# A gated cross-attention block on one core: first sample in whole float32 products, raw operands loaded where their low halves go, new engine orders

## The chip, the cores and the metric

One core of one Trainium2 chip runs the whole kernel. The metric is the device time of one execution in microseconds, as the median of several runs. A profiled execution of the same kernel gives the rows that are read below.

## What is computed

Eight samples of `x` and `ctx`, each 256 rows of 1024 values (C = 256, D = 1024), all float32, with small weights. Cut to what matters:

```
xn = layernorm(x)                                  # over the 1024 values
t  = Wt @ ctx ;  p = Wp @ xn ;  g = Wg @ ctx       # (256,256) @ (256,1024)
att = sum over a group of 32 rows of p*g           # one number per group and sample
y  = Wz (block diagonal) @ (att * t)
x1 = x + tanh(g_xattn) * (groupnorm(y)*gn_w + gn_b + ctx)
h  = layernorm(x1)
scores = (h @ Wq.T) @ keys.T                       # 64 experts
gate   = softmax over the 16 best scores, 0 for the others
z   = (h @ A.T) , gated expert by expert (8 columns each)
out = x1 + tanh(g_ffn) * 2 * (z_gated @ B.T)
```

## The kernel before, in words

The kernel rewrites the algebra. `Wu` (the product of Wz and Wt) is made once, and so is a router block (Wq and keys), 64 columns wide, which is put beside the 512 columns of A. Per sample n there are these products on PE:

- `u_product`: Wu times ctx, four uses of 512 columns into `w_ps[0..3]`; `gram`: x times ctx, transposed copies of both as operands, 256 by 256; `ctx_sums`: column sums of ctx; `n_product`: Wp times the corrected gram (`M`); `group_means` and `group_att_var`: averages over groups of 32 rows.
- `hT`: transposes of the attention result for the two row tiles t = 0, 1; `z_product(t, n)`: 8 chunks k of A with the router; `zT`: transposes of the gated z; `out_product(k, n)`: four quarters, each 4 chunks j of B.

A large product is made of three products of float32r operands: every operand v is held as v_hi (v rounded to float32r, by ACT: `xT_high`, `cT_high`, `c_high`, `lot_high`, `M_high`, `hT_high`, `zT_high`) and v_lo = v - v_hi (by DVE or POOL: `xT_low`, `cT_low`, `c_low`, `lot_low`, `M_low`, `hT_low`, `zT_low`), and hi*hi, hi*lo and lo*hi are summed in PSUM. `lot_high(j)` and `lot_low(j)` split one of 16 lots of 128x512 weights, 8 of A and 8 of B (KD = 8, KN = 4). Raw values arrive by DMA in places shared among several tensors: `raw`, `stage` and the working tiles `uw`.

DVE also computes the statistics (`x_stats`, `u_statistics`, `att_reduce`, `group_deviation`, `slopes`), the combination `w_tiles` of attention and residual, the gate (`gate`, a chain of some 11 small operations), `offsets` and the last addition `add_out`. POOL does low halves, the three powers of -1/2 (`x_root`, `y_root`, `w_root`), `x_shift` and `x_add`. ACT also does `u_copy`, `w_square`, `residual`, `scale_ctx` and `exps`.

The order is written out by hand for every engine, each engine being a fixed list that waits on semaphores. The list has a start (sample 0 alone, up to `hT(1, 0)`), a loop over b = 0..6 in which sample b's feed-forward part and sample m = b+1's attention part are interleaved (with b = 0 in special branches, since the weights' lots are still being split), and an end (sample 7 alone). On PE a round of the loop begins with `z_product(0, b)` at L872 and ends with `out_product(3, b)` at L899. SP issues all large DMAs in one queue in program order; a wait of SP holds back every later load.

Names and lines: `load_xT` L172, `load_cT` L179, first transposes L183 and L184, `load_x` L190, `load_c` L196, `load_lot` L213 and L216, POOL's `xT_low` L276, `cT_low` L281, `c_low` L287, `x_add` L299, `y_root` L307, `w_root` L311 and L313; ACT's `xT_high` L358, `cT_high` L364, `c_high` L370, `u_copy` L395, `w_square` L408, `hT_high` L414, `lot_high` L442; DVE's `lot_low` L532, `x_plus_ctx` L540, `x_stats` L547, `w_tiles` L629, `offsets` L633 to L636, `hT_low` L642, `gate` L653 to L677, `add_out` L687, `Wp_lo` L719, the router block's low half L731; PE's `gram` L790, `ctx_sums` L803, `u_product` L821, `n_product` L833, `group_means` L841, `group_att_var` L846, `hT` L860, `z_product` L872, `zT` L886, `out_product` L899, Wu L910, router L916.

The waits of PE's start, which the change replaces:

```
pe.wait_ge(wu_lo_s, 1)
u_product(0)
ctx_sums(0)
gram(0, lambda: None)
group_means(0)
pe.wait_ge(wp_lo_s, 1)
n_product(0)
group_att_var(0)
pe.wait_ge(router_lo_s, 1)
hT(0, 0)
hT(1, 0)
```

## Time and profile before

| | us |
|---|---|
| median of 3 runs (range) | 371.48 (370.81 to 372.13) |
| the profiled execution, device time | 369.46 |
| its span, first to last instruction | 367.6 |
| PE, DVE, ACT, POOL busy in the span | 336.3, 285.3, 159.8, 151.1 |
| start of `z_product(0, 1)`, from which the rounds repeat | 99.48 |

The span is 1.9 us shorter than the device time of the same execution, and that execution is 2.0 us faster than the median. The page's chain of waits puts 75% of the span on PE. In a row of a timeline, a record that says x8 is eight instructions, the first number is when the first starts and the second how long they take together; PE's records overlap, so that the distance from start to start is what a matmul costs. A matmul of whole float32 operands is two records, one of float32r operands is one.

### The profile page before, as it was taken

What the parts mean: (1) busy time and instruction counts of PE and PEld (TensorE: products, weight loads), DVE (VectorE), ACT (ScalarE), POOL (GpSimd) and SP (SyncE); (2) the same over time, 40 slices, a digit from 0 to 9 for tenths busy, and PEclk for the clock granted to TensorE, in tenths of its full rate; (3) what the DMA queues carried; (4) which work ended last, traced back from release to release, by engine and by line L of the source; (5) the groups of instructions that cost most, each with busy time, mean ns of one, the idle gap of its engine ahead of it and who ended that gap; (6) DMA issues with size and microseconds to landing.
All of it is one profiled execution on the core that took longest, in us unless ns stands there. A gap on an engine that the chain in (4) does not pass through costs nothing.

```text
span 367.6 us, 5693 instructions
## 1 busy us (share of the span) xinstructions
PE 336.3 (91%) x2104; PEld 307.9 (84%) x2104; DVE 285.3 (78%) x670; ACT 159.8 (43%) x257; POOL 151.1 (41%) x98
## 2 busy tenths in 40 slices
PE   5972996939699999999999999999999999999996
PEld 5871886728599889988999889988998899988984
DVE  2986489987868896898869896889689895787352
ACT  4690391751823445417612563344541761136110
POOL 0061178524476164553477067526455248000000
PEclk9995698978999999999999999999999999999999
DMA  7970571064721445062804173153606240001102
GB/s 265 406 263 32 203 256 57 0 235 123 247 84 57 171 157 189 0 229 75 270 3 156 74 220 126 59 171 139 206 1 230 67 164 0 2 1 59 57 29 87
DMA packets 14924, 47.50 MB, mean 129 GB/s; under 512 B 1824, under 2 KB 1952, under 8 KB 14896
## 3 DMA queue, kind: packets, MB, share of 16 engines
q1 hardware_dynamic: 14544, 46.93, 36.4%
q8 instruction: 17, 0.28, 0.3%
q10 hardware_dynamic: 352, 0.20, 0.2%
q14 instruction: 11, 0.09, 0.1%
HBM read 38.74 MB, written 8.39 MB: 128 GB/s over the span
## 4 chain that ended last, share of the span: by engine, by line
PE 75%; DVE 12%; DMA 5%; ACT 3%; issue 2%; POOL 1%; SPq 1%; ACTq 0%; DVEq 0%
PE w_ps L899 23%; PE z_ps L872 23%; PE w_ps L790 9%; PE w_ps L821 9%; PE t_ps L860 4%; DVE B_lo L532 3%; PE z_ps L833 3%; DMA uw<-in_cT 3%; PE w_ps L872 2%; PE t_ps L886 2%; DMA raw<-in_xT 1%; DVE u_st L581 1%; DMA raw<-in_cT 1%; PE t_ps L803 1%; DVE x_st L547 1%
## 5 line engine op out<-in xcount | busy, mean ns | idle before, releaser
L276 POOL TENSOR_TENSOR xT_lo<-raw,xT_hi 128x1024 fp32r<-128x1024 f32 x14 | 41.9, 3014 | 37.6 <-ACT xT_hi L358 37.6
L899 PE MATMUL w_ps<-B_hi,zT_hi 128*128 128x512 f32 x128 | 53.5, 418 | 2.4 <-issue 2.4
L899 PE MATMUL w_ps<-B_hi,zT_lo 128*128 128x512 f32 x128 | 50.7, 396 | 0.0
L899 PE MATMUL w_ps<-B_lo,zT_hi 128*128 128x512 f32 x128 | 50.6, 395 | 0.0
L872 PE MATMUL z_ps<-A_hi,hT_hi 128*128 128x288 f32 x224 | 49.2, 302 | 0.0
L872 PE MATMUL z_ps<-A_lo,hT_hi 128*128 128x288 f32 x224 | 48.7, 300 | 0.0
L872 PE MATMUL z_ps<-A_hi,hT_lo 128*128 128x288 f32 x224 | 48.5, 298 | 0.0
L872 PEld LDWEIGHTS z_ps<-A_hi,hT_hi 128*128 128x128 f32 x224 | 37.1, 193 | 0.6
L872 PEld LDWEIGHTS z_ps<-A_hi,hT_lo 128*128 128x128 f32 x224 | 36.8, 192 | 0.0
L872 PEld LDWEIGHTS z_ps<-A_lo,hT_hi 128*128 128x128 f32 x224 | 36.7, 192 | 0.0
L281 POOL TENSOR_TENSOR cT_lo<-raw,cT_hi 128x1024 fp32r<-128x1024 f32 x12 | 28.7, 2392 | 16.6 <-DVE uw L629 16.6
L434 ACT ACTIVATE ex<-sc,neg_max 128x64 f32<-128x64 f32 x16 | 5.6, 348 | 65.6 <-DVE neg_max L657 65.6
L287 POOL TENSOR_TENSOR c_lo<-c_sb,c_hi 128x1024 fp32r<-128x1024 f32 x14 | 33.6, 2424 | 0.0
L307 POOL TENSOR_TENSOR y_rs<-y_ve,minus_half 128x2 f32<-128x2 f32 x8 | 5.9, 740 | 65.6 <-DVE y_ve L616 65.6
L395 ACT ACTIVATE uw<-w_ps,neg_u 128x512 f32<-128x512 f32 x32 | 20.0, 685 | 26.5 <-DVE neg_u L586 26.5
L642 DVE TENSOR_TENSOR hT_lo<-t_ps,hT_hi 128x512 fp32r<-128x512 f32 x32 | 20.6, 683 | 12.7 <-ACT hT_hi L414 12.7
L899 PEld LDWEIGHTS w_ps<-B_hi,zT_hi 128*128 128x128 f32 x128 | 24.5, 191 | 7.1 <-issue 2.5
L414 ACT ACTIVATE hT_hi<-t_ps 128x512 fp32r<-128x512 f32 x32 | 17.5, 595 | 28.3 <-PE t_ps L860 28.3
L899 PEld LDWEIGHTS w_ps<-B_hi,zT_lo 128*128 128x128 f32 x128 | 24.4, 191 | 5.4
L899 PEld LDWEIGHTS w_ps<-B_lo,zT_hi 128*128 128x128 f32 x128 | 24.6, 192 | 4.2
L790 PE MATMUL w_ps<-cT_hi,xT_hi 128*128 128x256 f32 x96 | 27.6, 288 | 0.0
L860 PE MATMUL t_ps<-ident,uw 128*128 128x128 f32 x128 | 18.5, 292 | 9.5 <-DVE A_lo L731 5.7
(147 smaller groups left out, 868.7 us busy)
## 6 DMA issues: line engine op xcount, KB each, us to landing
c_sb<-in_ctx SPq DMA_DIRECT2D x16, 512.0 KB, 4.5
raw<-in_xT SPq DMA_DIRECT2D x16, 512.0 KB, 5.3
x_sb<-in_x SPq DMA_DIRECT2D x16, 512.0 KB, 3.2
out_block<-uw SPq DMA_DIRECT2D x14, 512.0 KB, 2.9
raw<-in_cT SPq DMA_DIRECT2D x12, 512.0 KB, 4.0
uw<-in_cT SPq DMA_DIRECT2D x4, 512.0 KB, 7.9
raw<-in_aT SPq DMA_DIRECT2D x4, 256.0 KB, 5.8
raw<-in_bT SPq DMA_DIRECT2D x4, 256.0 KB, 4.3
```

The source lines that it names most:

```text
L276: pool.tensor_tensor(xT_lo[:, half_of(h), :], raw[:, half_of(h), :], xT_hi[:, half_of(h), :].bitcast(f32), ALU.subtract).then_inc(xT_lo_s, 1)
L281: pool.tensor_tensor(cT_lo[:, half_of(h), :], raw_ctx(n)[:, half_of(h), :], cT_hi[:, half_of(h), :].bitcast(f32), ALU.subtract).then_inc(c ...
L287: pool.tensor_tensor(c_lo[:, t, :], c_sb[:, t, :], c_hi[:, t, :].bitcast(f32), ALU.subtract).then_inc(c_lo_s, 1)
L395: act.activation(uw[n % 2][:, t, cols], w_ps[k][:, :], ACT.Identity, bias=neg_u[:, t:t + 1]).then_inc(u_copied, 1)
L414: act.activation(hT_hi[:, t, g * HALF:(g + 1) * HALF], t_ps[g][:, :], ACT.Copy).then_inc(hT_hi_s, 1)
L532: dve.tensor_tensor(lo, slot(j), hi.bitcast(f32), ALU.subtract).then_inc(lot_lo_s, 1)
L642: dve.tensor_tensor(hT_lo[at], t_ps[g][:, :], hT_hi[at].bitcast(f32), ALU.subtract).then_inc(hT_lo_s, 1)
L790: last = pe.matmul(gram_bank(n, t)[:, 0:C], a[:, k, t * P:(t + 1) * P], c[:, k, :], start=(k == 0 and a is xT_hi and c is cT_hi), stop=(k ...
L821: last = pe.matmul(w_ps[k][:, :], w[:, c, rows], v[:, c, cols], start=(c == 0 and w is Wu_hi and v is c_hi), stop=(c == T - 1 and w is Wu_lo))
L860: last = pe.transpose(t_ps[g][:, k * P:k * P + P], uw[n % 2][:, t, d:d + P], ident[:, :])
L872: last = pe.matmul(banks[i][:, 0:ZH], h[:, t, row], w[:, k, i * ZH:(i + 1) * ZH], start=(k == 0 and h is hT_hi and w is A_hi), stop=(k == ...
L899: last = pe.matmul(w_ps[k][:, :], z[:, t, row], w[:, j, cols], start=(j == 0 and z is zT_hi and w is B_hi), stop=(j == KN - 1 and z is zT_lo))
```

## The change

- Places: the helper `split` gives v_hi a place of its own and lets the raw values and v_lo share one, for A, B, Wp, xT and cT; the low half overwrites its raw values. `xT_first` and `cT_first`, sample 0's transposes, lie where B_hi will be. `c_sb` is two buffers, used alternately. `raw` is gone.
- Sample 0's `u`, `gram` and `n` become single products of whole float32 operands (`first_u`, `first_gram`, `first_n`), with neither hi nor lo halves of ctx, xT, cT, M; Wu and Wp are split later, for sample 1.
- PE: the router's products move behind the first gram, sample 1's `u_product` moves into the start, behind `first_n`; `hT(1, 0)` goes inside `z_product(0, 0)`; round 0 is written out with `n_product(1)` behind `out_product(0, 0)`.
- POOL: low halves in pieces of 512 columns; it splits lots 4 to 7 of A and 0 to 3 of B, DVE the rest. In the rounds, `xT_low` and `cT_low` are interleaved and `cT_low` no longer waits for `w_done`.
- SP: most waits go. Transposes of sample n are loaded once gram(n-1) is done, since their place holds that gram's low halves.
- DVE: `offsets` goes behind the additions of a round.

The diff, cut to its core:

```diff
+        def split(name, shape):
+            hi = sb(f"{name}_hi", shape, f32r)
+            with nc.sbuf_tensor(f"{name}_in", shape, f32) as raw:
+                pass
+            return hi, sb(f"{name}_lo", shape, f32r), raw
...
+            def load_transposes(n):
+                for h in range(NH):
+                    if n >= 2 and h == 0:
+                        sp.wait_ge(gram_done, per_tile(n - 1, T - 1))
+                    sp.dma_start(xT_raw[:, half_of(h), :], xT[n][:, half_of(h), :]).then_inc(xT_in[h], 16)
+                    sp.dma_start(cT_raw[:, half_of(h), :], cT[n][:, half_of(h), :]).then_inc(cT_in[h], 16)
             def load_c(n):
-                    if n > 0:
-                        sp.wait_ge(w_done, per_tile(n - 1, t))
+                    if n > 1:
+                        sp.wait_ge(w_done, per_tile(n - 2, t))
...
             load_c(0)
+            load_x(0)
             load_first_transposes()
-            load_x(0)
+            load_c(1)
...
-            for j in range(KD - 2):
+            for j in range(KD):
                 load_lot(j)
-            load_cT(0, 1)
-            for j in range(KD - 2, KD):
+            load_transposes(1)
+            for j in range(KD, KD + KN):
                 load_lot(j)
             load_x(1)
-            load_xT(1)
-            load_c(1)
-            load_cT(1, 1)
-            for j in range(KD, N_LOTS):
+            for j in range(KD + KN, N_LOTS):
                 load_lot(j)
-            load_xT(2)
+            load_c(2)
             for b in range(NB - 1):
                 if b + 2 < NB:
+                    load_transposes(b + 2)
                     load_x(b + 2)
-                    load_cT(0, b + 2)
-                    load_cT(1, b + 2)
-                    load_c(b + 2)
-                store(b, 0)
                 if b + 3 < NB:
-                    load_xT(b + 3)
-                store(b, 1)
+                    load_c(b + 3)
+                for t in range(T):
+                    store(b, t)
...
             pool.wait_ge(w_done, per_tile(0, T - 1))
+            for j in range(KH, KD):
+                lot_low(j)
             xT_low(0, 1)
+            w_root(0)
+            cT_low(0, 1)
             xT_low(1, 1)
-            w_root(0)
...
+            cT_low(1, 1)
+            for j in range(KD, KD + KN):
+                lot_low(j)
+            x_root(1)
+            x_add(1)
+            y_root(1)
+            pool.wait_ge(w_done, per_tile(1, T - 1))
+            xT_low(0, 2)
+            w_root(1)
+            cT_low(0, 2)
+            xT_low(1, 2)
+            cT_low(1, 2)
+            for m in range(2, NB):
                 x_root(m)
                 c_low(m)
...
+                x_shift(m)
+                if m + 1 < NB:
+                    xT_low(0, m + 1)
+                    cT_low(0, m + 1)
+                y_root(m)
+                if m + 1 < NB:
+                    xT_low(1, m + 1)
                 w_root(m)
-                if nn < NB:
-                    cT_low(1, nn)
+                if m + 1 < NB:
+                    cT_low(1, m + 1)
...
(ACT)
+            act.wait_ge(wu_done, 1)
+            act.activation(Wu_first[:, :, :], ..., ACT.Copy).then_inc(wu_s, 1)
             c_high(0, 0)
             c_high(1, 0)
-            for h in range(NH):
-                xT_high(h, 0)
-                cT_high(h, 0)
...
+            cb_copy(0)
+            scale_ctx(0)
+            for t in range(T):
+                c_high(t, 1)
+            u_copy(0)
+            M_high(0)
...
+            for j in range(KD):
                 lot_high(j)
+            xT_high(0, 1)
+            cT_high(0, 1)
+            xT_high(1, 1)
             hT_high(0, 0)
+            w_square(0)
+            cT_high(1, 1)
+            ...Wp_hi...
+            hT_high(1, 0)
+            u_copy(1)
+            exps(0, 0)
+            act.wait_ge(gram_done, per_tile(0, T - 1))
+            for j in range(KD, KD + KN):
+                lot_high(j)
+            exps(1, 0)
+            zT_high(0, 0)
+            cb_copy(1)
+            scale_ctx(1)
+            M_high(1)
+            for j in range(KD + KN, N_LOTS):
+                lot_high(j)
+            residual(0)
+            zT_high(1, 0)
...
(DVE)
+            lot_low(0)
+            att_reduce(0)
+            lot_low(1)
+            slopes(0, lambda: lot_low(2))
+            w_tiles(0)
+            hT_low(0, 0)
+            lot_low(3)
+            u_statistics(1)
+            hT_low(1, 0)
+            offsets(0)
+            gate(0, 0)
+            ...Wp_lo...
+            x_stats(1)
+            minus_means(1)
+            gate(1, 0, w_ps[NH:USES])
+            zT_low(0, 0)
+            gram_fix(1)
+            M_low(1)
+            group_deviation(1)
+            for j in range(KD + KN, N_LOTS):
                 lot_low(j)
+            att_reduce(1)
+            zT_low(1, 0)
+            slopes(1)
+            w_tiles(1)
...
(PE)
+            first_u()
+            ctx_sums(0)
+            first_gram()
+            group_means(0)
+            ...router...
+            first_n()
+            u_product(1, lambda: group_att_var(0))
             pe.wait_ge(router_lo_s, 1)
             hT(0, 0)
-            hT(1, 0)
-            for b in range(NB - 1):
+            z_product(0, 0, z_ps, lambda: hT(1, 0), KN - 2)
+            pe.wait_ge(u_copied, per_use(1, USES - 1))
+            z_product(1, 0, w_ps[NH:USES])
+            zT(0, 0)
+            gram(1, lambda: ctx_sums(1))
+            group_means(1)
+            out_product(0, 0)
+            n_product(1)
+            zT(1, 0)
+            out_product(1, 0, lambda: group_att_var(1))
+            out_product(2, 0, lambda: hT(0, 1))
+            out_product(3, 0, lambda: hT(1, 1))
+            for b in range(1, NB - 1):
```

## Rows read from the trace of the kernel before

**Rows 1.** Windows: PE, PEld, DVE, ACT, POOL busy (count), PEclk, DMA share, GB/s.

```profile
99.48:139.38 39.90, 39.90 (x263) 36.88 (x262) 33.73 (x81) 17.90 (x30) 20.38 (x12) 1.00 0.37 126
...
339.21:367.60 28.39, 24.99 (x153) 22.23 (x151) 10.77 (x36) 3.28 (x6) 0.00 (x0) 1.00 0.15 56
```

**Rows 2.** Windows of the start: all of it, and four us within it.

```profile
0.00:99.48 99.48, 71.54 (x394) 64.30 (x395) 76.45 (x155) 52.65 (x82) 40.05 (x30) 0.86 0.54 190
...
12.00:16.00 4.00, 4.00 (x16) 3.24 (x16) 3.90 (x4) 2.21 (x3) 0.00 (x0) 1.00 1.03 409
```

**Rows 3.** PE's waits in the whole span: us in total, times, longest.

```profile
PE t_ps L860 <- DVE A_lo L731: 5.7, 1, 5.7
...
PE t_ps L886 <- DVE zg_sb L677: 3.7, 1, 3.7
```

**Rows 4.** PE's timeline: start, us, what [idle before <-releaser].

```profile
4.13 2.04 PE L910 MATMUL z_ps<-uw 128*128 128x128 f32 x8 [4.13 <-DMA uw<-in_wzT]
6.28 3.64 PE L916 MATMUL t_ps<-stage 16*128 16x64 f32 x16
9.85 0.80 PE L821 MATMUL w_ps<-c_hi,Wu_hi 128*128 128x512 f32 x1
...
12.58 0.63 PE L821 MATMUL w_ps<-c_hi,Wu_hi 128*128 128x512 f32 x1
...
13.57 0.39 PE L821 MATMUL w_ps<-c_hi,Wu_hi 128*128 128x512 f32 x1
...
25.64 0.35 PE L833 MATMUL z_ps<-M_hi,Wp_hi 128*128 128x256 f32 x1 [2.19 <-DVE M_lo L573]
...
35.48 1.97 PE L860 MATMUL t_ps<-ident,uw 128*128 128x128 f32 x8 [5.71 <-DVE A_lo L731]
...
44.07 0.42 PE L872 MATMUL z_ps<-A_hi,hT_hi 128*128 128x288 f32 x2
```

**Rows 5.** The chain that ended last: start, us, what.

```profile
30.69 1.09 POOL y_rs L307
...
99.48 6.37 PE z_ps L872 x48
105.85 2.87 PE w_ps L790 x24
108.73 0.44 PE t_ps L803 x4
...
118.86 5.46 PE w_ps L821 x24
124.33 1.43 PE z_ps L833 x12
...
127.92 5.59 PE w_ps L899 x24
...
205.65 0.44 PE t_ps L886 x4
```

**Rows 6.** DVE's timeline.

```profile
38.73 0.68 DVE L532 TENSOR_TENSOR A_lo<-raw,A_hi 128x512 fp32r<-128x512 f32 x1
...
55.07 2.00 DVE L670 TENSOR_TENSOR g_scale<-g_rec,w_rs 128x1 f32<-128x1 f32 x1
...
57.91 5.48 DVE L532 TENSOR_TENSOR B_lo<-stage,B_hi 128x512 fp32r<-128x512 f32 x2
63.31 0.27 DVE L653 TENSOR_SCALAR sc<-w_ps,w_rs 128x64 f32<-128x64 f32 x1
...
65.51 0.88 DVE L677 SCALAR_TENSOR_TENSOR zg_sb<-w_ps,g_scale,eg 128x288 f32<-128x288 f32 x2
...
205.22 0.21 DVE L583 BATCH_NORM_AGGREGATE u_mv<-u_st 128x2 f32<-128x12 f32 x1
```

**Rows 7.** POOL's timeline.

```profile
52.35 4.71 POOL L281 TENSOR_TENSOR cT_lo<-uw,cT_hi 128x1024 fp32r<-128x1024 f32 x2 [1.95 <-ACT cT_hi L364]
```

**Rows 8.** ACT's timeline.

```profile
24.84 1.15 ACT L442 ACTIVATE A_hi<-raw 128x512 fp32r<-128x512 f32 x2
```

More of the change, by code:

```diff
@@ L762, in _ @@
                 w_tiles(m)
-                offsets(m)
                 add_out(0, b)
@@ L769, in _ @@
                 add_out(3, b)
+                offsets(m)
             gate(0, NB - 1)
@@ L779, in _, with first_gram @@
         def _(pe):
+            def first_gram():
+                for t in range(T):
+                    for k in range(KD):
+                        if k % KH == 0 and t == 0:
+                            pe.wait_ge(first_xT_in[k // KH], 16)
+                            pe.wait_ge(first_cT_in[k // KH], 16)
+                            if k == 0:
+                                pe.wait_ge(wu_s, 1)
+                        last = pe.matmul(gram_bank(0, t)[:, 0:C], xT_first[:, k, t * P:(t + 1) * P], cT_first[:, k, :],
+                                         start=(k == 0), stop=(k == KD - 1))
+                    last.then_inc(gram_done, 1)
             def gram(n, between):
@@ L805, in ctx_sums, with first_u, u_product @@
                 last.then_inc(cb_done, 1)
-            def u_product(n):
-                if n >= 2:
-                    pe.wait_ge(M_lo_s, per_tile(n, T - 1))
+            def first_u():
+                pe.wait_ge(wu_s, 1)
+                for k in range(USES):
+                    t, cols = use(k)
+                    for c in range(T):
+                        if k == 0:
+                            pe.wait_ge(c_in[c], 16)
+                        last = pe.matmul(w_ps[k][:, :], Wu_first[:, c, t * P:(t + 1) * P], c_sb[0][:, c, cols],
+                                         start=(c == 0), stop=(c == T - 1))
+                    last.then_inc(u_done, 1)
+            def u_product(n, middle=None):
+                if n == 1:
+                    pe.wait_ge(wu_lo_s, 1)
+                else:
+                    pe.wait_ge(M_lo_s, from_second(n, T - 1))
                 for k in range(USES):
@@ L824, in u_product, with first_n @@
                     last.then_inc(u_done, 1)
+                    if k == 0 and middle:
+                        middle()
+            def first_n():
+                pe.wait_ge(wp_in, 16)
+                pe.wait_ge(M_hi_s, per_tile(0, T - 1))
+                for t in range(T):
+                    for c in range(T):
+                        last = pe.matmul(z_ps[0][:, t * C:(t + 1) * C], Wp_raw[:, c, t * P:(t + 1) * P],
+                                         M_first[:, c, :], start=(c == 0), stop=(c == T - 1))
+                last.then_inc(n_done, 1)
             def n_product(n):
-                pe.wait_ge(M_lo_s, per_tile(n, T - 1))
-                if n > 0:
+                pe.wait_ge(M_lo_s, from_second(n, T - 1))
+                if n == 1:
+                    pe.wait_ge(wp_lo_s, 1)
+                else:
                     pe.wait_ge(zg_done, per_tile(n - 1, T - 1))
@@ L874, in z_product @@
                                              stop=(k == KD - 1 and h is hT_lo))
-                    if gated and k == KD - 3:
+                    if gated and k == at:
                         gated()
```

363 lines of the change are left out of this document (140 added, 223 removed).

## The prediction

> **What bounds the kernel now.** I read the windows first. From 99.48 us on, the kernel repeats a round of 39.9 us in which PE is busy for all of it, six times, and then ends in 28.4 us with 25.0 of PE [rows 1]. Nothing in those rounds waits for anything but PE, and the change takes no product out of them. What it can give back lies before 99.48: there PE is busy 71.5 us of 99.5, and its mean clock is 0.86 [rows 2], which is time at the lower of its two levels (1.2 and 2.4 GHz). The waits name what PE lacked: the low half of the router block before the first transposes, 5.7 us; sample 0's gated z, 3.7 us [rows 3]. PE's timeline shows the start in order: Wu's products end at 6.2, `u_product(0)` begins at 9.85 and runs at the lower clock until about 13.2 (0.63 us a record at 12.58, 0.39 at 13.57), `n_product(0)` begins at 25.64 after a wait of 2.2, the first transposes at 35.48 after 5.7, at the lower clock again, which lasts until 44.07 [rows 4]. So the question is when `z_product(0, 1)` can begin, which is 99.48 now.
>
> **Prices.** At the higher clock two float32 matmuls of 128 columns are four records in 0.44 us (L803 [rows 5]), 0.22 a matmul; 512 columns cost four times that, 0.87, and 256 columns 0.44; at the lower clock twice as much. Three float32r matmuls of 512 columns cost 3 x 5.46/24 = 0.68, the gram's three of 256 columns 3 x 2.87/24 = 0.36 [rows 5]. The whole-value products thus cost 8 x 0.19 + 16 x 0.08 + 4 x 0.08 = 3.1 us more of PE; they save no PE time, only the waits for halves. A 512-column copy on ACT takes 0.58 us [rows 8], a 1024-column one twice that; a low half of 1024 columns on POOL 2.36 [rows 7], a piece of 512 1.2 (estimate, half of it; unsplit overhead could make it 1.4); a lot's low half on DVE 0.68 when nothing is in its way, as at 38.73 [rows 6]. `z_product` is 6.4, `out_product` 2.8, `n_product` 1.4, `zT` 0.4 [rows 5]; eight transposes took 1.97 at the lower clock [rows 4], so 1.0.
>
> **The start, step by step** (us from the span's start).
> 1. ACT copies Wu as its first work: 6.2 + 0.6 + a little = 6.9, against 9.85 before, since the router's products (3.64) and the halves of Wu and ctx no longer stand ahead. `first_u` is eight matmuls. In the trace the clock rose some 3.5 us after dense work began at 9.85, and 8.6 after 35.48, where transposes with gaps came first [rows 4]. I take 4: 4.1 us at 1.74 do 2.4 matmuls, 5.6 more cost 4.9: end at 15.9 (15.3 for a rise at 10; 20.8 with none).
> 2. `ctx_sums` 0.4, `first_gram` 16 x 0.44 = 7.0: 23.3. The gram ended at 23.4 before (25.64 less its wait), so the early start pays just for the dearer matmuls. The first transposes land behind x now; at 409 GB/s [rows 2] the 1 MB more ahead of them is 2.6 us, and they are not wanted before 16.3.
> 3. `group_means` 0.4 and the router at half of 3.64 = 1.8: 25.5. M takes that time anyway (wait of 2.2 before). `first_n` 1.8: 27.3.
> 4. `u_product(1)` 5.5 with `group_att_var(0)` (0.4) in it: 33.2. Under it runs the chain that was bare before: variance, POOL's power (1.09 [rows 5]), slope, then `w_tiles` 2 x 1.3, first tile by 32.7, second by 33.9. This moves 5.5 us of `u_product(1)` into PE's holes and keeps the clock up.
> 5. `hT(0, 0)` 1.0: 34.2. ACT reaches it late: router copy from 25.5, eight lots 4.6, three copies of 1024 columns 3.4, so 34.2; copy 0.6, DVE's low half 0.7: `z_product(0, 0)` begins at 35.7, PE idle 1.5.
> 6. 6.4 and `hT(1, 0)` 1.0: 43.1. POOL's lots 4 to 7 run from 33.9, 4 x 1.2 = 38.7, wanted from about 39.8: hidden by a us.
> 7. `z_product(1, 0)` wants `u_copy(1)`: on ACT 1.2 + 2.3 + 1.1 + 0.6 + 1.2 + 2.3 after 34.2, about 43: no wait. End 49.5.
> 8. `zT` 0.4, gram(1) and its sums 6.2: 56.1. Its halves on POOL are three and a half further low halves and `w_root`, ready at 49.2.
> 9. DVE: gate(0, 0) from 43.1, 3.1 us when free (63.31 to 66.4 [rows 6]) and up to 2 x 1.2 of blocking, 48.6; Wp's low half, `x_stats` and its small ones 4.0, 52.6; gate(1, 0) 3.1 + 2.0, 57.7; `zT_low` 0.7: `out_product(0, 0)` begins at 58.4, PE idle 1.9.
> 10. 2.8 + 1.4 + 0.4 + half an `out_product` 1.4: 64.4. DVE: M 2.0, deviation 0.6, lots 12 to 15 4 x 1.0, `att_reduce` 0.8: 65.8, PE idle 1.4. Then 0.3 and 2.8: 68.9.
> 11. Slope by 68.1, first tile 69.4: idle 0.5. `hT(0, 1)` 1.0 and 2.8: 73.2. ACT squares until 72.9, copy and low half until 74.2: idle 1.0; 1.0 and 1.4 more: `z_product(0, 1)` begins at **76.6**, 22.9 earlier. Idle in all 6.3, the uncertain term: 0 if nothing blocks, twice if everything is late.
>
> **Blocking between DVE and POOL.** A small DVE operation, one column wide, took 2.00 us at 55.07, and two lots took 5.48 at 57.91 instead of 1.36, both while POOL made low halves of 1024 columns [rows 6, 7]. The change halves POOL's pieces, so a blocked operation should lose up to 1.2 rather than 2.4, but gives POOL eight lots more; `offsets` moves off the way before the transposes.
> The Trainium skill, page SBUF — State Buffer, section Who interferes with whom, says that a DVE instruction with two SBUF inputs and a GpSimd instruction that reads SBUF exclude each other, whoever starts first keeping the port for its whole instruction. The trace agrees as far as it goes, and the rule speaks against giving POOL more.
>
> **The rounds.** POOL has 20.4 us of work in 39.9 [rows 1] and gets at most six more instruction starts; SP loads sample m+1's transposes only after gram(m), 12.6 into the round; 2 MB at 409 GB/s is 5.1, with issue some 20; ACT copies at 20.6 to 22.6 behind `exps(1, b)`, POOL's two first low halves 21.6 to 26.4; `y_root` is wanted at 29.3. Next late would be `y_root` and with it `hT(0, m)`; cover 2.9 there and some 2 more behind. But these low halves now collide with gate(1, b) and the mean's chain: u's statistics ended at 205.43 and PE wanted them at 206.1 [rows 5, 6], 0.7 of cover against a block of 1.2. Bounds 0 and 0.8 a round; I take 0.3, nearer the free end as only one or two operations can be hit, over five rounds 1.5. A gain there is excluded: PE has no idle time in them. The end is unchanged.
>
> **Sum.** -22.9 + 1.5 = -21.4. The profiled execution took 369.46 (span 367.6): 348.1. The median is 2.0 above it: 371.5 - 21.4 = **350.1**.
>
> **Rivals.**
> - Blocking as often as it can (0.16). Some ten two-input operations stand on DVE between 43 and 66; if each waits out a piece, 12 us instead of my 6, PE's start of the round moves to about 82: 355.5. For it: 57.91. Against: POOL has gaps after 56.
>   By the rule on the Trainium skill's page SBUF — State Buffer (section Who interferes with whom) this is what steady POOL work brings.
> - Dense float32 does not raise the clock (0.07). `first_u` ends at 20.8, sums and gram double to 15: 35.7, `first_n` too; 13 us later than in step 3, then float32r work raises it: 363. For it: no row shows a rise within float32 work. Against: PE streams without a gap there.
> - **Slower** (0.04): the shared place of raw and low halves. If the transposes come so late that POOL's pair ends after y's variance, `y_root`, `w_tiles` and `hT(0, m)` slide, and PE idles each of five rounds. It decides when the pair ends after about 31 instead of 26.4; to eat 22.9 us it must lose 4.6 a round, the pair ending near 36, loads 9 us later than worked out: 373. Against: the queue is 0.37 busy in a round [rows 1].
> - Forecast as above, idle between 0 and 12 (0.73).
>
> **Range and chances.** Below: no idle at all would give 343.8. Above: the first rival with 0.6 a round more reaches 358.5. The second rival and the slower one stay out, 0.11, and some of the tails. A measurement tells 0.3% (1.1 us) from no change. Faster 0.95, same 0.01, slower 0.04.
>
> **What would show it.** Right: `z_product(0, 1)` begins at 74 to 80; float32 records of `first_u` change pace near 11; gram(0) ends near 23; no clock at 0.5 after; six intervals of 39.9 to 40.7. Wrong: records of the first gram 0.44 us apart instead of 0.22 (second rival); DVE operations of small tiles above 1.2 us in a row (first); a round above 42 with POOL's power as releaser (slower).

## The result, and the profile after

The changed kernel takes 345.36 us (median of 4 runs, 345.08 to 345.52), the kernel before, on the same chip, 371.14 us (370.39 to 372.13): a ratio of 0.930, 95% interval 0.928 to 0.933. The profiled execution took 345.4 us, its span is 343.6 us, 24.0 less than before.

The page of the kernel after: busy time of each engine, the clock in 40 slices (here and above as its column gives it), and the chain that ended last, by engine.

```profile
PE 331.4 (96%) x2076; PEld 298.6 (87%) x2076; DVE 253.6 (74%) x656; ACT 155.1 (45%) x254; POOL 155.7 (45%) x148
...
PEclk9999999999999999999999999999999999999999
...
PE 85%; POOL 9%; issue 2%; ACT 1%; DVE 1%; DMA 1%; POOLq 0%; DVEq 0%
```

PE is busy 96% of the span. Before, it was 336.3 of 367.6, or 91%. So its work fell by 5 us, which I read as less time at the lower clock (the mean granted clock of the whole execution is 0.963 before and 1.000 after), less what whole values cost, and its idle time by 19. The chain is on PE for 85% instead of 75%.

The windows, columns as in [rows 1]: the start, two rounds, the end.

```profile
0.00:75.39 75.39, 66.55 (x366) 55.09 (x367) 56.94 (x138) 48.17 (x79) 42.62 (x44) 1.00 0.70 255
75.39:115.37 39.98, 39.98 (x262) 36.88 (x262) 33.35 (x81) 17.93 (x30) 25.52 (x23) 1.00 0.39 134
115.37:155.35 39.98, 39.98 (x262) 36.87 (x262) 30.85 (x81) 17.86 (x30) 19.51 (x18) 1.00 0.38 132
315.25:343.60 28.35, 24.97 (x153) 22.24 (x151) 11.07 (x39) 4.08 (x6) 0.00 (x0) 1.00 0.15 56
```

All of the gain is in the first row. The start took 99.48 us [rows 2] and takes 75.39; the six rounds took 239.73 us (99.48 to 339.21) and take 239.86 (75.39 to 315.25), the end 28.39 and 28.35 [rows 1]. DMA share times length is 54 us before and 53 us now: the same bytes, packed closer. The first round still has 2.5 us more of DVE work and 6 of POOL's than a later one.

PE's waits, all that the view lists: us in total, times, longest.

```profile
PE z_ps L964 <- DMA uw<-in_wzT: 4.4, 1, 4.4
PE w_ps L953 <- DVE zT_lo L653: 1.8, 1, 1.8
PE z_ps L926 <- DVE hT_lo L648: 1.0, 1, 1.0
PE w_ps L839 <- ACT products L448: 0.7, 1, 0.7
PE t_ps L899 <- DVE att_var L597: 0.7, 1, 0.7
PE t_ps L913 <- DVE uw L635: 0.3, 1, 0.3
```

The waits of [rows 3], 5.7 for the router block's low half and 3.7 for sample 0's gated z, are gone. What is left after Wu is 4.5 us in all.

PE's timeline of the start (some rows of it; those of `first_n`, `hT` and later group several records):

```profile
26.35 1.97 PE L872 MATMUL z_ps<-zg_sb,Wp_in 128*128 128x256 f32 x8
27.97 0.58 PE L859 MATMUL w_ps<-c_hi,Wu_hi 128*128 128x512 f32 x1
...
33.90 1.03 PE L913 MATMUL t_ps<-ident,uw 128*128 128x128 f32 x8
35.91 0.53 PE L926 MATMUL z_ps<-A_hi,hT_hi 128*128 128x288 f32 x2 [0.98 <-DVE hT_lo L648]
...
49.65 0.60 PE L940 MATMUL t_ps<-ident,zg_sb 128*128 128x128 f32 x4
...
58.54 0.50 PE L953 MATMUL w_ps<-B_hi,zT_hi 128*128 128x512 f32 x1 [1.80 <-DVE zT_lo L653]
...
69.11 1.09 PE L913 MATMUL t_ps<-ident,uw 128*128 128x128 f32 x8 [0.33 <-DVE uw L635]
...
75.22 0.43 PE L926 MATMUL z_ps<-A_hi,hT_hi 128*128 128x288 f32 x2
```

Two rows of `first_u` alone, split where the records' pace changes (columns: PE busy with its count, PEld busy, PEclk, DMA share, GB/s):

```profile
7.10:12.90 5.80, 5.80 (x7) 2.52 (x8) 1.00 1.03 397
12.90:17.00 4.10, 4.10 (x10) 1.52 (x8) 1.00 1.02 411
```

Seven records in the first 5.8 us are 0.83 us each, ten in the next 4.1 us are 0.41 (one lies on the cut): by their pace the lower level, then the higher. The PEclk column says 1.00 in both, so at the start the pace of the records has to be read, not the column.

Who holds up the start? The chain of waits over that stretch, by line, for the kernel before and then the kernel after (the view cuts the row off):

```profile
by line: DVE B_lo L532 11.6%; DMA uw<-in_cT 9.7%; issue 8.4%; DMA raw<-in_xT 5.3%; DVE u_st L581 4.9%; PE w_ps L899 4.3%; DMA raw<-in_cT 3.9%; PE t_ps L860 3.2%; DVE x_st L547 2.4%; POOL xT_lo L276 2.4%; ACT stage L408 2.3%; DVE g_scale L67
```

```profile
by line: PE w_ps L839 13.1%; PE z_ps L798 9.2%; issue 8.5%; POOL A_lo L267 7.3%; POOL cT_lo L260 7.3%; POOL xT_lo L260 6.6%; POOL B_lo L267 6.6%; POOL c_sb L293 6.6%; PE w_ps L953 5.5%; ACT A_hi L445 4.8%; DMA uw<-in_wzT 4.7%; DVE uw L635 3
```

Before, loads of transposes are 18.9% of 99.48 us, 18.8 us. In order of time they are these:

```profile
3.56 9.69 DMA uw<-in_cT
39.81 5.25 DMA raw<-in_xT
88.25 3.87 DMA raw<-in_cT
```

The first is sample 0's, issued at 3.56 without a wait for any place. Only the other two, 9.1 us, were held back until a shared place came free. After, the one load in the chain is `wzT`, 3.5 us.

The chain after must be read with care: it passes through POOL's low halves only across 4.66 us of "issue" from 62.15. POOL's own timeline shows what it waited for there:

```profile
66.84 0.70 POOL L303 TENSOR_TENSOR y_rs<-y_ve,minus_half 128x2 f32<-128x2 f32 x1 [4.69 <-DVE y_ve L622]
```

It was DVE. So the shares of `A_lo`, `xT_lo`, `cT_lo` and `B_lo` do not show that POOL holds up the start; what PE itself waits for is what the list of waits says, DVE's results.

### The profile page after: what moved, and what is told of

It reads as the page before. It is cut to its first block, busy times and chain, and to the rows that moved or that the text cites. A ratio compares the mean times of both kernels' runs of the same rounds, so it can differ in the third digit from the quotient of the medians.

```text
span 343.6 us, 5669 instructions
## 1 busy us (share of the span) xinstructions
PE 331.4 (96%) x2076; PEld 298.6 (87%) x2076; DVE 253.6 (74%) x656; ACT 155.1 (45%) x254; POOL 155.7 (45%) x148
## 4 chain that ended last, share of the span: by engine, by line
PE 85%; POOL 9%; issue 2%; ACT 1%; DVE 1%; DMA 1%; POOLq 0%; DVEq 0%
PE z_ps L926 24%; PE w_ps L953 24%; PE w_ps L814 10%; PE w_ps L859 10%; PE t_ps L913 4%; PE w_ps L839 3%; PE z_ps L885 3%; PE z_ps L798 2%; PE w_ps L926 2%; PE t_ps L940 2%; POOL A_lo L267 2%; POOL cT_lo L260 2%; POOL xT_lo L260 1%; POOL B_lo L267 1%; POOL c_sb L293 1%
## 5 line engine op out<-in xcount | busy, mean ns | idle before, releaser
L260 POOL TENSOR_TENSOR xT_lo<-xT_in,xT_hi 128x512 fp32r<-128x512 f32 x28 | 35.6, 1295 | 48.9 <-ACT xT_hi L358 46.1
L953 PE MATMUL w_ps<-B_hi,zT_hi 128*128 128x512 f32 x128 | 52.8, 413 | 1.8 <-DVE zT_lo L653 1.8
L926 PE MATMUL z_ps<-A_hi,hT_hi 128*128 128x288 f32 x224 | 48.5, 298 | 1.0 <-DVE hT_lo L648 1.0
L926 PEld LDWEIGHTS z_ps<-A_hi,hT_hi 128*128 128x128 f32 x224 | 36.3, 189 | 1.8 <-DVE hT_lo L648 1.2
L260 POOL TENSOR_TENSOR cT_lo<-cT_in,cT_hi 128x512 fp32r<-128x512 f32 x28 | 36.1, 1312 | 0.0
L279 POOL TENSOR_TENSOR c_lo<-c_sb,c_hi 128x512 fp32r<-128x512 f32 x24 | 30.1, 1287 | 0.0
L953 PEld LDWEIGHTS w_ps<-B_hi,zT_hi 128*128 128x128 f32 x128 | 24.1, 188 | 6.4 <-DVE zT_lo L653 2.3
L953 PEld LDWEIGHTS w_ps<-B_lo,zT_hi 128*128 128x128 f32 x128 | 24.1, 189 | 4.1
L814 PE MATMUL w_ps<-cT_hi,xT_lo 128*128 128x256 f32 x96 | 27.1, 283 | 0.0
L814 PE MATMUL w_ps<-cT_lo,xT_hi 128*128 128x256 f32 x96 | 27.1, 283 | 0.0
L659 DVE TENSOR_SCALAR sc<-z_ps,w_rs 128x64 f32<-128x64 f32 x14 | 4.0, 284 | 31.0 <-PE z_ps L926 30.4
L693 DVE SCALAR_TENSOR_TENSOR uw<-w_ps,tg,uw 128x512 f32<-128x512 f32 x32 | 23.2, 743 | 4.5 <-PE w_ps L953 4.3
```

The source lines that it names most:

```text
L260: last = pool.tensor_tensor(lo[:, chunks, :], came[:, chunks, :], hi[:, chunks, :].bitcast(f32), ALU.subtract)
L279: last = pool.tensor_tensor(c_lo[:, t, cols], c_sb[n % 2][:, t, cols], c_hi[:, t, cols].bitcast(f32), ALU.subtract)
L693: dve.scalar_tensor_tensor(uw[n % 2][:, t, cols], w_ps[k][:, :], tg2[:, 0:1], uw[n % 2][:, t, cols], ALU.mult, ALU.add).then_inc(out_added, 1)
L814: last = pe.matmul(gram_bank(n, t)[:, 0:C], a[:, k, t * P:(t + 1) * P], c[:, k, :], start=(k == 0 and a is xT_hi and c is cT_hi), stop=(k ...
L926: last = pe.matmul(banks[i][:, 0:ZH], h[:, t, row], w[:, k, i * ZH:(i + 1) * ZH], start=(k == 0 and h is hT_hi and w is A_hi), stop=(k == ...
L953: last = pe.matmul(w_ps[k][:, :], z[:, t, row], w[:, j, cols], start=(j == 0 and z is zT_hi and w is B_hi), stop=(j == KN - 1 and z is zT_lo))
```

## The experiments

All were timed beside the kernel before. "z(0,1)" is the start of `z_product(0, 1)`, read from the chain, 75.39 in the kernel after. The gain of the start is called by its suspected parts: u in the gap, pieces, clock, whole values, the late loads as a danger.

**u_late**: sample 1's `u_product` goes back behind gram(1), and with it `u_copy(1)` on ACT and `u_statistics(1)` on DVE; the rest stays.

```diff
-            u_product(1, lambda: group_att_var(0))
+            group_att_var(0)
...
             gram(1, lambda: ctx_sums(1))
+            u_product(1)
             group_means(1)
```

> The changed kernel with sample 1's u product put back behind gram(1), so that nothing stands under sample 0's chain from n to the first transposes. Theory A (the gain is work of sample 1 moved into PE's holes): PE idles 4 to 5.5 us before the first transposes at about 33.9, the clock may fall, and 5.5 us of u come back after gram(1), of which the 1.8 us wait for zT_low covers a part: 349 to 353 us. Theory B (the gain is the whole-value products of sample 0, which are unchanged here): within 1 us of 345.4. Theory C (most of the gain is the clock): 352 to 357, as z_product(0, 0) would run at the lower clock again.

349.54 us (348.86 to 350.65), ratio 0.941 (0.939 to 0.944): 4.2 slower than the kernel after. z(0,1) at 79.34. The waits that come back:

```profile
PE t_ps L915 <- DVE uw L635: 4.0, 2, 3.7
...
PE t_ps L895 <- DVE u_mv L587: 1.0, 1, 1.0
...
```

```profile
26.00:39.00 13.00, 7.77 (x37) 6.83 (x36) 8.70 (x19) 11.57 (x19) 6.76 (x6) 0.74 1.04 400
```

PE is busy 7.8 of 13 us there, at a clock of 0.74 (waits first, then the window of 26 to 39 us). So `u_product(1)` in the gap is worth 4 us, part as filled idle time, part as clock: theory A's range, at its lower end.

**single_ctx**: as u_late, and each load of ctx waits for the sample before, as in the kernel before, at its old place in SP's queue; the halves of sample 1's ctx are made later accordingly.

```diff
-                    if n > 1:
-                        sp.wait_ge(w_done, per_tile(n - 2, t))
+                    if n > 0:
+                        sp.wait_ge(w_done, per_tile(n - 1, t))
```

> Edit: the part two ctx buffers undone in effect: each load of ctx waits until the sample before it has used its tiles, as in the kernel before, at the place in SyncE's queue that it had there. The second sample's u product then can't stand in the gap of the first and goes behind gram(1), as in the run called u_late (349.5 us); its two high halves on ScalarE and low halves on VectorE move to 40 to 46 us. Theory A (the second buffer is worth what the u product in the gap is worth, and nothing in the rounds): 349.5 us to 352 us, with the rounds at 39.98 us. Rival B (the late ctx loads are worth much by themselves: they land behind the weights' lots, and the 4.6 us of low halves fall on a VectorE that is busy there): 353 to 358 us, with a wait of TensorE of 3 us or more for u or the sums of ctx near 53 us. Rival C (they cost in the rounds): rounds over 40.3 us.

353.54 us (352.00 to 355.01), ratio 0.953 (0.948 to 0.958): 8.2 slower than after and 4.0 slower than u_late by the medians; z(0,1) at 82.00, the next round 39.96. Its four runs fall in two pairs, 352.0 and 352.1, 355.0 and 355.0. The profiled one is of the faster pair, and beside u_late's it is 2.7 slower, in the time and in z(0,1). So the late loads of ctx cost some 2.5 us beyond u_late in the faster pair and 5.5 in the other.

```profile
...
PE t_ps L894 <- DVE u_mv L586: 2.5, 1, 2.5
PE w_ps L860 <- DVE zg_sb L682: 1.0, 1, 1.0
```

The median lies in rival B's range and the faster pair at the top of A's. By the waits it is nearer to B, though not by B's own sign: the waits for u's statistics and for gated z are 3.5 us, not one wait of 3, and they come from DVE, where the two low halves of ctx now take 3.7 us at 48.0. Rival C is out: the second buffer costs or gives nothing in the rounds. I read its worth as this, that ctx is there early, so that both its low halves and `u_product(1)` fit where DVE and PE are free.

**whole_pieces**: POOL's low halves of ctx and of the transposes and `x_add` in instructions of 1024 columns again; the weights' lots stay at 512.

```diff
-                return [slice(i * HALF, (i + 1) * HALF) for i in range(NH)]
+                return [slice(0, D)]
...
-                for i in range(2):
-                    chunks = slice(h * KH + 2 * i, h * KH + 2 * i + 2)
+                for chunks in (half_of(h),):
```

> The changed kernel with POOL's low halves and x_add in instructions of 1024 columns again (lots stay at 512). Theory D (blocking by the length of POOL's instruction): DVE's blocked operations in the start, which lose some 8 us in all at up to 1.1 us each, lose up to 2.3 each; those between 49 and 58 us go straight into PE's wait for zT_low: 346.5 to 348.5, and DVE operations of a few columns that take 2 us or more. Theory A (only the work's place counts): within 0.6 us of 345.4.

353.11 us (352.36 to 354.31), ratio 0.953 (0.949 to 0.957): 7.8 slower, far above what I had expected. The trace says how. DVE's timeline of whole_pieces:

```profile
78.98 2.26 DVE L638 TENSOR_TENSOR kappa<-gnb_t,beta 128x2 f32<-128x2 f32 x1
81.16 2.43 DVE L639 TENSOR_TENSOR kappa<-u_dev,slope 128x2 f32<-128x2 f32 x1
...
90.14 2.00 DVE L675 TENSOR_TENSOR g_scale<-g_rec,w_rs 128x1 f32<-128x1 f32 x1
```

And POOL's and PE's at the same time:

```profile
78.81 2.42 POOL L259 TENSOR_TENSOR xT_lo<-xT_in,xT_hi 128x1024 fp32r<-128x1024 f32 x1
81.16 2.41 POOL L259 TENSOR_TENSOR cT_lo<-cT_in,cT_hi 128x1024 fp32r<-128x1024 f32 x1
```

```profile
93.11 0.66 PE L939 MATMUL t_ps<-ident,zg_sb 128*128 128x128 f32 x4 [2.35 <-DVE zg_sb L682]
```

```profile
93.70:101.70 8.00, 8.00 (x50) 7.99 (x49) 4.07 (x6) 1.17 (x3) 0.63 (x1) 0.79 0.94 327
```

Two operations of two columns, 0.19 and 0.14 us in the kernel after, took 2.26 and 2.43, each until POOL's instruction ended; `g_scale` took 2.00 instead of 0.94. DVE was so late in the gate that PE waited 2.35 us in the first round, and after that wait its clock was 0.79 over 8 us. That makes 4.3 us (the first round took 44.31 us instead of 39.98), and the start is 2.8 later as well (PE's first record of `z_product(0, 1)` at 78.04 instead of 75.22), with new waits of PE of 0.9 us before `first_n` and 1.6 before `group_means(1)`. After the first round each is 40.10 instead of 39.98. POOL's work itself is cheaper in whole instructions (2.40 for 1024 columns, 2 x 1.30 in pieces). So the piece's length sets what one collision costs, and it counts in the start and in the first round's gate.

**before_pieces**: the kernel before with POOL's work in pieces of 512.

```diff
-                pool.tensor_tensor(xT_lo[:, half_of(h), :], raw[:, half_of(h), :], ...
+                for i in range(2):
+                    chunks = slice(h * KH + 2 * i, h * KH + 2 * i + 2)
+                    last = pool.tensor_tensor(xT_lo[:, chunks, :], raw[:, chunks, :], ...
```

> The kernel before with POOL's low halves and x_add in instructions of 512 columns, nothing else. In its start DVE operations lose about 18 us to blocking (for instance 2.2 of 2.35, 2.1 of 2.32, 4.1 of 5.48), and with the holes filled it hardly gained, so its start hangs on DVE's chain. Theory D: half of the blocking that lies on the chain goes, 365 to 369. Theory A: PE's order and the serial loads bind, 370 to 372.

367.60 us (366.49 to 369.06) against 371.17, ratio 0.993 (0.990 to 0.996): 3.6 faster than before, in theory D's range; z(0,1) is at 97.20 instead of 99.48, 2.3 earlier in the profiled executions. Pieces alone give 3.6 us before and 7.8 in the new order. That the new order leaves DVE and PE less slack, and that a late DVE there also costs the clock, is my reading of the difference; no run separates the two.

**lots_dve**: all 16 low halves of lots on DVE, none on POOL.

```diff
-            for j in range(KH, KD):
-                lot_low(j)          # POOL
...
-            lot_low(3)
+            for j in range(3, KD):
+                lot_low(j)          # DVE
...
+            for j in range(KD, KD + KN):
+                lot_low(j)
```

> The changed kernel with all 16 lots' low halves on DVE, none on POOL. Theory A: DVE's chain is what PE waits for at two places. Four lots of A (2.7 us) before u_statistics(1) delay hT_low(1, 0) and the mean of u, four of B (2.7 us) go straight into the wait for zT_low: 348 to 351. Theory D (blocking between DVE and POOL is what costs, so less on POOL is better): 345.4 or less.

346.73 us (346.12 to 347.10), ratio 0.933 (0.931 to 0.936): 1.4 slower.

```profile
PE w_ps L925 <- ACT uw L393: 1.3, 1, 1.3
...
PE t_ps L892 <- ACT cb_sb L377: 0.6, 1, 0.6
```

Two waits of 1.3 and 0.6 us are new, that for `u_copy(1)` on ACT among them, and one of 0.5 for B's low half. z(0,1) is at 76.59, 1.2 later, though `first_u` took 8.68 us instead of 9.90 in this execution. So POOL's share of the lots is worth 1.4 by the medians and at most 2.4 by these rows, less than the 3 to 6 I gave it. Theory D, no loss at all, is out as well.

**gram_three**: sample 0's gram as three products of halves again; ACT makes four high and DVE four low halves for it.

```diff
-                        last = pe.matmul(..., xT_first[:, k, ...], cT_first[:, k, :],
-                                         start=(k == 0), stop=(k == KD - 1))
+                        for a, c in ((xT_hi, cT_hi), (xT_hi, cT_lo), (xT_lo, cT_hi)):
+                            last = pe.matmul(..., a[:, k, ...], c[:, k, :], ...
```

> The changed kernel with sample 0's gram made of three float32r products of split operands, its raw transposes in the places of sample 1's. ACT's four copies and DVE's four low halves go into the idle stretch from 9.7 to 17.5 us. Theory A: PE saves 16 x (0.43 - 0.36) = 1.1 us of gram, the halves are ready at 18.7 for the second half of the chunks, sample 1's transposes still land before ACT wants them near 31: 344 to 346. Theory B (whole values are what helps, since splits stand in the way): 4 us or more slower, gram(0) ends at 27 or later.

347.63 us (347.40 to 347.96), ratio 0.936 (0.935 to 0.938): 2.3 slower, between the two expectations. PE's timeline:

```profile
22.32 0.28 PE L903 MATMUL t_ps<-u_mv,group_mean 128*128 128x2 f32 x2
22.53 1.99 PE L986 MATMUL t_ps<-stage 16*128 16x64 f32 x16
25.74 3.75 PE L882 MATMUL z_ps<-zg_sb,Wp_in 128*128 128x256 f32 x8 [1.22 <-ACT zg_sb L386]
```

DVE's timeline:

```profile
20.84 3.43 DVE L724 TENSOR_TENSOR c_lo<-c_sb,c_hi 128x1024 fp32r<-128x1024 f32 x2
24.19 0.87 DVE L575 SCALAR_TENSOR_TENSOR z_ps<-cb_sb,neg_x,z_ps 128x256 f32<-128x256 f32 x2
```

The gram ends at 22.3, 1.9 us earlier than with whole values (0.7 of it because `first_u` took 9.18 us in this execution instead of 9.90), but its correction on DVE (the second row) stands behind the low halves of sample 1's ctx, which end at 24.2, as they end at 24.8 in the kernel after. So M is hardly earlier, PE idles 1.22, and then `first_n` takes 3.75 us instead of 1.97, at a granted clock of 0.50. Whole values save no time on PE; they keep it busy while DVE and ACT do other things. The edit also holds sample 1's transposes back until this gram is done; PE's later waits are those of the kernel after (1.0 for `hT`, 1.8 for `zT`), so that costs nothing that shows.

**before_filled**: the kernel before, with 108 filler matmuls where PE idles in the start, their results unused.

```diff
+            def fill(count, bank):
+                for i in range(count):
+                    pe.matmul(bank[:, 0:C], Wu_hi[:, 0, 0:P], Wu_hi[:, 1, :], start=True, stop=True)
```

> The kernel before with filler matmuls (float32r, 256 columns, into idle banks, results unused) in the holes of its start: 42 in the hole before the first transposes, 24 before zT(0, 0), 42 around group_means(1). All waits stay as they were; only the clock is kept up. Theory C: most of the 24 us is the clock, so this reaches 355 or less. Theory A: the low stretches cost half of about 8 us at 35 to 44, 3 at 58 to 61 and 4 at 81 to 85, less what the waits behind take back: 364 to 368.

369.62 us (367.50 to 371.35, 10 runs) against 371.27, ratio 0.996 (0.994 to 0.999).

```profile
0.00:100.81 100.81, 81.20 (x501) 73.49 (x502) 76.95 (x155) 54.01 (x85) 40.15 (x30) 0.97 0.54 191
```

The clock of the start is 0.97 instead of 0.86 [rows 2], PE is busy 81 us instead of 72, and z(0,1) is at 100.81 (this execution is the slowest of the ten). By the medians the clock alone gives 1.7 us, less than either theory gave it: with PE faster, it only waits longer for DVE, ACT and the loads. So the 24 us are not a matter of the clock alone. The fillers held nothing up where they stand: before the first transposes PE still waits 1.5 us for DVE, before `zT(0, 0)` 1.0, before `group_means(1)` 0.5.

**warm**: the kernel after, with 6 filler matmuls of whole float32 before Wu and 2 before `first_u`.

```diff
+            pe.wait_ge(ident_done, 1)
+            for i in range(6):
+                pe.matmul(t_ps[1][:, 0:P], ident[:, :], ident[:, :], start=True, stop=True)
             pe.wait_ge(wt_in, 16)
...
+            for i in range(2):
+                pe.matmul(t_ps[1][:, 0:P], ident[:, :], ident[:, :], start=True, stop=True)
             first_u()
```

> The changed kernel with six filler matmuls of float32 (128 columns) on PE before the first weights land and two between Wu and first_u, results unused. In the changed kernel the first 6.8 of 16 records of first_u run at the lower clock, until 12.9 us, which costs 2.9 us. If the rise comes a fixed time after dense work begins, it comes 2.7 us earlier and saves 1.4: 344.0. If it comes at a time of its own, no difference: 345.4. Theory C, by which the clock decides elsewhere too, would not change this number.

343.08 us (342.57 to 345.26), ratio 0.927 (0.922 to 0.932): 2.3 faster than after by the medians, where 1.4 was expected; the intervals of the two ratios overlap, so the size is uncertain.

```profile
6.91 7.36 PE L839 MATMUL w_ps<-c_sb,products 128*128 128x512 f32 x16
...
21.67 1.99 PE L980 MATMUL t_ps<-stage 16*128 16x64 f32 x16
23.63 2.93 PE L872 MATMUL z_ps<-zg_sb,Wp_in 128*128 128x256 f32 x8
```

`first_u` takes 7.36 us instead of 9.90. In this execution, the slowest of its four (345.26), part was lost again behind the router's thin products: PE did not wait, and still `first_n` took 2.93 instead of 1.97 (granted clock 0.68 from 23.6 to 26.0).

**late_loads**: the slower rival made real. From sample 2 on, the transposes' loads also wait for the `z_product(1, ...)` that follows the gram.

```diff
                         sp.wait_ge(gram_done, per_tile(n - 1, T - 1))
+                        sp.wait_ge(z_done, per_tile(n - 2, T - 1))
```

> The changed kernel, in which sample m+1's transposes wait in every round also for z_product(1, m-1), 6.8 us later than gram(m) (19.4 into the round instead of 12.6). The cover worked out in the prediction is 4.6 us for POOL's pair of low halves before y_root is late: by it ACT's first copy moves from 20.6 to about 23.5, the pair ends near 30 instead of 26.4, and a round loses 0 to 1.5 us: 345.4 to 353. If there is no such cover, each of five rounds loses the 6.8: 379. If the loads have much more room than that, 345.4.

355.28 us (354.65 to 357.85), ratio 0.960 (0.955 to 0.965): 9.9 slower, in rounds of 41.95, 42.20 and 41.94 us; 0 to 1.5 a round and at most 353 in all were expected. z(0,1) is untouched, 75.53.

```profile
PE w_ps L954 <- ACT uw L398: 4.8, 5, 1.5
...
```

```profile
141.45 1.06 ACT L359 ACTIVATE xT_hi<-xT_in 128x1024 fp32r<-128x1024 f32 x1 [3.35 <-DMA xT_in<-in_xT]
144.00 1.06 ACT L365 ACTIVATE cT_hi<-cT_in 128x1024 fp32r<-128x1024 f32 x1 [1.49 <-DMA cT_in<-in_cT]
144.96 2.41 ACT L398 ACTIVATE uw<-w_ps,neg_u 128x512 f32<-128x512 f32 x4
```

The waits come first, then ACT's timeline in a round that begins at 117.48. The first load is issued 19.46 us into the round instead of 12.60, 6.9 later, and that costs 2.0 to 2.2 a round. If a delay beyond the cover counts in full, the cover in the kernel after is 4.6 to 4.9 us (an estimate from this one delay; no second one was tried). What is late is ACT: it waits 3.35 and 1.49 us for the loads, and `u_copy` of the sample, which PE's `out_product` needs, stands behind the two copies. POOL's `y_root` still waits 1.43 us for DVE, at 31.6 us into the round: it is not what decides. The delay was mis-priced, and the instruction too.

**wp_behind, router_within, three_edits**: attempts on the waits that are left. Wp's low half behind `M_low(1)`; the router's products one by one between the gram's; both, with the fillers of warm.

```diff
-            dve.wait_ge(wp_hi_s, 1)          # Wp_lo
...
             M_low(1)
+            dve.wait_ge(wp_hi_s, 1)          # Wp_lo, three lines
```

```diff
                         last = pe.matmul(gram_bank(0, t)[:, 0:C], xT_first[:, k, ...], cT_first[:, k, :], ...)
+                        if t == 1:
+                            r = pe.matmul(t_ps[0][:, k * NE:k * NE + NE], wq_sb[:, k * P:k * P + P], keys_sb, ...)
```

> Edit: the low half of Wp (one DVE instruction, 0.95 us at 48.13 in the profile of the changed kernel) is moved from in front of the statistics of x of the second sample to behind M_low(1). Theory A (the start is a chain on VectorE that ends at zT_lo, for which TensorE waits 1.8 us before out_product(0,0)): the wait falls to about 0.85 us and the kernel gains 0.95 us, 344.4 us. Rival B (what is gained there only moves to the next wait, for att_var or uw, since DVE then is as late at 66 us as before): 345.2 to 345.6 us, no change. n_product(1) needs the low half only after out_product(0,0), 5.8 us of matmuls, so it should not wait.

> Edit: the 8 thin matmuls of the router (16 records of 64 columns on 16 partitions, 1.99 us between the gram of the first sample and first_n) are put one by one between the matmuls of the gram's second tile. Their work is unchanged. The M that first_n waits for then is ready about 2 us later relative to TensorE's last work, so A (the start is bound by TensorE's own work, and M is ready 1 us or more before first_n asks): the same 345.4 us, within 1. B (the router covers the chain from the gram's end to M, and out of its place that chain is bare; the router's own time in the gram pushes M 2 us later): TensorE waits 1 to 2.5 us before first_n and, after such a gap, runs first_n and part of the u product at the lower clock: 347 to 350 us.

> Edit: both of the above (Wp's low half later, the router within the gram), and the filler matmuls of the run called warm (343.1 us). Sum of the parts if they are independent: 345.4 - 2.3 (warm) - 0.95 (Wp) + what the router within the gram gives. With A for both: 342 us. If the router was needed in its place (B): 344 to 346 us.

wp_behind: 344.93 us (343.76 to 347.52), ratio 0.929 (0.925 to 0.933), not told from the kernel after, and so between A's 344.4 and B's 345.2 to 345.6 without deciding. Its waits for `zT_lo`, `att_var` and `uw` are 1.5, 0.8 and 0.4 us instead of 1.8, 0.7 and 0.3, 0.1 less in all where A had 0.95: Wp's low half takes 1.17 at its new place and the small operation behind it 1.07, both beside POOL. By these waits it is rival B. The profiled execution is the slowest of the four, with z(0,1) at 77.51, and what makes it slow is the clock, in a place that the edit does not touch:

```profile
26.62 3.56 PE L872 MATMUL z_ps<-zg_sb,Wp_in 128*128 128x256 f32 x8
```

`first_n` took 3.56 us instead of 1.97 behind the router's products, with no wait before it, and `first_u` 10.12.

router_within: 347.87 (347.51 to 350.48), ratio 0.939 (0.935 to 0.944), 2.5 slower, in the range of B, but not by B's clock:

```profile
22.64 0.43 PE L804 MATMUL t_ps<-stage 16*128 16x64 f32 x2
...
23.63 0.43 PE L804 MATMUL t_ps<-stage 16*128 16x64 f32 x2
...
27.85 1.97 PE L880 MATMUL z_ps<-zg_sb,Wp_in 128*128 128x256 f32 x8 [0.51 <-ACT zg_sb L387]
```

The rows show thin records and `first_n`; the gram's two records stand between the thin ones. A pair of thin records and a pair of gram records cost 0.99 us from start to start; apart, the router's two cost 0.25 and the gram's two 0.43, so the switch costs 0.3 us a turn, 8 times, 2.5 us. The wait before `first_n` is 0.51, and `first_n` keeps its 1.97. three_edits: 346.11 (345.79 to 346.75), ratio 0.933 (0.931 to 0.936): warm's gain less this loss. The lowest median stays warm's.

## Why the prediction was right, and where it was off

The forecast was 350.1 us, within 343.5 to 358.5; 345.36 came. The gain lies before `z_product(0, 1)`, as said, and by the steps that were named. From the span's start, forecast and timeline:

| | forecast | measured |
|---|---|---|
| 1: `first_u` ends | 15.9 | 16.8 |
| 2: first gram ends | 23.3 | 24.2 |
| 3: `first_n` begins, `u_product(1)` begins | 25.5, 27.3 | 26.35, 27.97 |
| 4, 5: `hT(0, 0)`; `z_product(0, 0)`, PE idle | 33.2; 35.7, 1.5 | 33.90; 35.91, 1.0 |
| 7: `zT(0, 0)` | 49.5 | 49.65 |
| 9: `out_product(0, 0)`, PE idle | 58.4, 1.9 | 58.54, 1.8 |
| 10, 11: idle for `att_var`, `uw`, `hT` | 1.4, 0.5, 1.0 | 0.7, 0.3, 0 |
| `z_product(0, 1)` | 76.6 | 75.39 |
| a round (mean of six before: 39.96) | 39.9 + 0.3 | 39.98 |

- **The start**, -22.9 forecast and -24.1 measured. Step 1 had the rise of the clock 4 us after dense work began; it took 5.8 us, which cost 0.9. Steps 3 and 4 gave back 0.2 and step 5's idle time was 0.5 shorter, so that steps 7 and 9 fit within 0.15 in part because two misses cancel, and steps 10 and 11 gave back the rest: 1.0 us of waits in place of 2.9, with 0.6 more of work. Idle in all was 3.8 us (the 0.7 for Wu's copy was in step 1), not 6.3. The wait named last, for `hT(1, 1)`, did not come. Two of the signs that were named came late: the pace of `first_u` changed at 12.9, not near 11, and gram(0) ended at 24.2, not near 23.
- **The rounds**, +1.5 forecast, +0.1 measured over the six intervals (239.86 against 239.73). In this term I had charged blocking to PE. It does take place: in the round from 115.37, `slope` took 1.23 us, the two tiles of `uw` 3.47 instead of 2.48, and `g_scale` 0.93. PE waits for none of them, and the mean's chain, which I feared for, begins at 142.58, half a us after POOL's pair ends. With 1024 columns (whole_pieces) a round did become 0.12 longer, and the first one 4 us.
- **The offset to the median**: the prediction set the sum on the profiled execution and added 2.0. Before, that execution was a low one (369.46, median 371.14 beside the kernel after); after, it is 345.4 beside 345.36. The offset was a matter of the kernel before: among its executions timed beside the experiments the five from 368.97 to 369.25 have a mean granted clock of 0.967 to 0.972, those above 371 one of 0.954 to 0.963 (one has 0.968), while the kernel after has 0.994 to 1.000 in all four. So some 2 us of the gain by the medians do not appear in the two profiles. The misses of 1.2 for the start, 1.4 for the rounds and 2.0 for the offset make up the 4.7 us between forecast and result.
- **The prices** held: whole float32 products cost what was worked out (gram 6.9 us against 7.0), and they save nothing themselves; gram_three shows the rest for the gram, that the work taken off ACT and DVE, with the clock behind it, is worth 2.3 us. `first_u` and `first_n` were not undone.
- **Blocking** was in the forecast as a term of some 6 us of idle and as a rival. By whole_pieces, the part of the change that I passed over in a sentence, the halved pieces, carries 7.8 us of the result. Without it the outcome would have been 353, near the rival's 355.5.
  The Trainium skill, page SBUF — State Buffer, section Who interferes with whom, says that a DVE instruction with two SBUF inputs contends with a GpSimd instruction that reads SBUF, and that the lock is exclusive. The trace agrees: `kappa`, with two inputs, starts at 78.98 and 81.16 in whole_pieces, and ends within 0.02 us of POOL's instructions of 2.42 and 2.41 us.
- **The slower rival** did not come: rounds stayed at 39.98. By late_loads the cover was 4.6 to 4.9 us against the 2.9 + 2 that I gave. Its mechanism was placed wrongly. I had `y_root` on POOL as what would be late; late_loads shows `u_copy` on ACT and, through it, PE, 2.0 to 2.2 us a round for 6.9 us of delay, while POOL still waited. The rival had 4.6 us of delay free and the rest in full; one delay cannot test that rule, since the cover above was worked out with it. The instruction that decides is another.
- **The dense float32 rival** is out: within `first_u`'s own records the pace doubled, and fillers of the same kind (warm) moved that almost to its start.

How the 24 us divide is only in part shown. Undone alone, the second ctx buffer with `u_product(1)` in the gap costs 8.2 us (4.2 of it the place of `u_product(1)`), the pieces 7.8, whole values in the gram 2.3, POOL's lots 1.4 (each against medians that spread by 0.4 to 3 us). These do not add up by right, since each falls on a start that has less slack than before. What raw values in the place of their low half give by themselves, with the loads that no longer wait, was not tried alone: the places and the orders hang together, and undoing the one needs the other. The evidence for it is the chain of waits above: before, 9.1 us of loads that were held back for a place, after, none. It stays an argument, and the part of the title's change that no run here shows by itself.

## What to carry to other kernels

A start that waits for raw values to leave a shared place is a chain through DMA, ACT, DVE and SP; making the load's place the one that its result will overwrite took it off that chain here at no space, though what that alone is worth was not measured. When an engine shares ports with another, the length of its longest instruction sets what a collision costs: cutting POOL's work in two cost 0.2 us of POOL per 1024 columns and gave 7.8 us here. Filling PE's gaps with the next sample's product was worth 4.2 us of a product of 5.5, but the clock alone, with fillers, was worth 1.7 us of 371, since other engines led.

## What the runs showed of the hardware that was not expected

- The PEclk column said 1.00 from 7.1 to 12.9 us while `first_u`'s records were 0.83 us each, twice the later pace.
- The clock fell after short idle times: 1.22 us behind the router's thin products in gram_three, 2.35 us in whole_pieces. After waits of 1.0 and 1.8 us in the kernel after, among dense products, it did not.
- Idle time is not needed for it to fall. Behind the same thin products `first_n` took 2.93 us in warm and 3.56 in wp_behind, with no wait before it, and 1.96 to 1.97 in the kernel after, u_late, lots_dve and late_loads; in whole_pieces it took 1.97 even after 0.89 us of idle. So in gram_three the idle time may not be the cause of the fall.
- The moment of the first rise differs between executions: `first_u`, the same sixteen records, took 9.90 us in the kernel after, 9.16 in u_late, 8.68 in lots_dve, 8.55 in router_within and 10.12 in wp_behind. Starts compared from one execution each are uncertain by 1 to 1.5 us for that alone; the medians are what the verdicts rest on.
- Changing between products of 16 partitions with 64 columns and of 128 partitions with 256 costs about 0.3 us a turn.
- A DVE operation of 128 x 2 values was held for a whole POOL instruction of 1024 columns: 2.43 us for 0.14.
